# Preparing a selective state-space step: half-width products placed up to three steps ahead, the time-step bias inside a product, the skip term as a diagonal product

## The chip, the cores and the metric

One core of one Trainium2 chip runs the whole kernel. The metric is device time in microseconds. The kernel before took 3630.87 us in the median of three runs (3621.93, 3630.87 and 3643.5 us).

## What is computed

A one-layer tower over ids of shape 2 x 2048: embedding (256 wide) and 16-head attention, then `h = h + mamba(layernorm(h))`, then `h = h + ffn(layernorm(h))`. The change lies in the second part, the Mamba block, which runs once forward and once over the reversed sequence and adds the two:

```python
xh, z = jnp.split(x @ in_w.T, 2, axis=-1)                  # 512 channels each
xc = silu(conv_b + sum(xp[:, k:k + L, :] * conv_w[:, k] for k in range(4)))
dt, Bm, Cm = split(xc @ xproj_w.T)                         # 16, 16, 16
delta = softplus(dt @ dt_w.T + dt_b)
deltaA = exp(einsum('bld,dn->bldn', delta, -exp(A_log)))
deltaBu = einsum('bld,bln->bldn', delta * xc, Bm)
h = dA * h + dBu;  y = einsum('bdn,bn->bd', h, c)           # scan over the sequence, 16 states
y = (ys + xc * D_param) * silu(z);  return y @ out_w.T
```

All of it is float32.

## The kernel before

The program has four parts one after the other: embedding and projections, attention, `attention_out_and_mamba`, and `mamba_out_and_ffn`. Only the third is touched. Its second block is the state-space stage.

**Work units.** The stage has 16 *steps*: two directions, two batch rows, four chunks of 512 positions. A step has 64 *tiles* (slots), tile t = 4n + i for state n (16) and channel group i (4 groups of 128 channels). For each tile, ScalarE writes `da` = exp(delta * A) (line 1282) and a quarter of `bu` (line 1267: the transposed `delta*xc` scaled by B, one 128x512 block of positions; the fourth block of every second state is made by VectorE, line 1303). TensorE transposes `bu` back into PSUM (`inject`, line 1211, four 128-column transposes). VectorE runs the scan (line 1322). GpSimd multiplies the result by C (line 1187). TensorE adds this to `ps_y` by four accumulating transposes (`add`, line 1223), four tiles later (`LAG`).

**Preparation of later steps.** Between tiles, the same engines prepare the next steps in *fills* of a two-bank PSUM buffer `ps_a`: XH (input projection to xh, line 816, 4 fills of two 512-column products), CONV (taps as diagonal products, line 834, 4 fills of three), PROJ (line 838, four products), BT (transposes of B), DELTA (the 16-row time-step product, line 847, 4 fills), Z (line 821, 4 fills of two), DUT (transposes of delta*xc, line 853, 4 fills), YT (transposes of the gated output, line 826). Each fill takes the bank of the fill two places before it in `order`, and waits until that bank has been evacuated (`evacuated`, lines 763 to 771): by VectorE for CONV and DELTA, by ScalarE for the others. VectorE adds the last tap (`take_conv`, line 932); ScalarE takes SiLU of xc and of z (`silu_x`, `silu_z`, with a table load before and after) and the softplus: VectorE first writes min(x + bias, 20) (`cap`, line 941), ScalarE takes Exp and Ln (lines 906, 908), VectorE joins max(x + bias, that) (line 948). GpSimd makes delta*xc (`make_du`, line 801) and the skip term xc*D (line 1196), which TensorE adds by four transposes (line 1230).

**The order is written out by hand.** `PE_AT`, `ACT_AT`, `DVE_AT` and `DU_AT` (lines 714 to 728) say after which tile of the running step each piece for the next step is issued on each engine; a slot below 0 lies a step earlier (slot k - 64 u). All engines run in order. What keeps them together: `inject(t)` waits for scan t-2 (two PSUM banks, line 1209), `da` has 9 buffers, `bu` three states (line 1266), `hs` 8, `g` 5. So ScalarE may run several tiles ahead of the scan and TensorE at most two. Pieces with a slot before the first tile run in a prologue, before the first scan.

Of the kernel before, what the change touches and what calls it, by code (L numbers as in the profile page):

```python
# [36 lines left out]
XPW = X_DT2 + R  # L37
# [582 lines left out]
NDA, NHS, NG, NBU = 9, 8, 5, 3  # L620
HB = DC - 1
LAG = 4
CQ = 2
CAP = 20.0


def attention_out_and_mamba(nc, sem, o_scr, wo, bo, h_scr, dirs, win_t, xp_t, dtw_t, xn_scr, y_scr, c_scr):

    with ExitStack() as ctx, ExitStack() as ctx_out, ExitStack() as ctx_steps:
# [15 lines left out]
        def where(s):  # L645
# [9 lines left out]
        cols = sb("cols", [P, 2, 3, ND], FP32)  # L655
        a_cur = sb("a_cur", [P, 2, ND, DS], FP32)
        taps = sb("taps", [P, 2, ND, DC - 1, P], FP32)
        xn = sb("xn", [P, 2, KD, CH], FP32)
        xh = sb("xh", [P, ND, HB + CH + HB], FP32)
        skip = sb("skip", [P, CH], FP32)  # L660
# [35 lines left out]
        capped, e_ok, ln_ok, halo_ok = s_("capped"), s_("e_ok"), s_("ln_ok"), s_("halo_ok")  # L696
# [11 lines left out]
        skip_ok, skipped = s_("skip_ok"), s_("skipped")  # L708
# [95 lines left out]
        def fill(s, j, part):  # L804
# [5 lines left out]
            if f >= NA and first:  # L810
                evacuated(nc.tensor, f - NA)
            if j < CONV:
# [3 lines left out]
                last = nc.tensor.matmul(bank, win[:, part, j * P:(j + 1) * P], xn[:, q, part], start=first, stop=final)  # L816
            elif Z <= j < DUT:
# [3 lines left out]
                last = nc.tensor.matmul(bank, xn[:, q, part, tb * P:(tb + 1) * P], win[:, part, DI:2 * DI], start=first, stop=final)  # L821
# [5 lines left out]
            elif j < YT:  # L827
# [783 lines left out]
```

## Time and profile before

| | |
|---|---|
| median of three runs | 3630.87 us |
| the profiled execution: its span (the page gives no other time of it) | 3653.6 us |
| state-space stage, first to last scan | 1684.2 to 3354.5 us |
| busy share of the whole span, TensorE / VectorE / ScalarE / GpSimd | 91% / 79% / 76% / 43% |
| one full step (the sixth) | 104.0 us |

The page of the profile gives busy time and the costliest groups of instructions. A timeline row is a start, a length, engine, line, operation, output<-input and, in brackets, the idle time before it with what ended it. "x3" is the number of instructions merged into one row. Matmul lengths are modelled and overlap; the distance of two starts is the better measure.

### The profile page before, as it was taken

The numbers are of one execution on the slowest core, as the hardware profiler recorded it, in microseconds if no ns is written. First come the engines' busy times: TensorE is split into PE (matmuls) and PEld (weight loads), VectorE is DVE, ScalarE is ACT, GpSimd is POOL, SyncE is SP. The second block draws the span as 40 slices with busy tenths as digits, with TensorE's granted clock in tenths as the row PEclk, the third lists the DMA queues.
The fourth block names the chain that finished last, engine by engine and source line by source line (L and its number), as shares of the span: only waits on it lengthen the run. The fifth ranks groups of instructions, "written<-read, shape, count | busy, mean of one in ns | idle before, by whom it ended". The sixth has DMA issues, their size and how long they took to land. (4 is left out here: it accounts for less than half of the span.)

```text
span 3653.6 us, 69996 instructions
## 1 busy us (share of the span) xinstructions
PE 3330.3 (91%) x23969; PEld 1934.0 (53%) x23969; DVE 2898.1 (79%) x2810; ACT 2784.4 (76%) x4727; POOL 1569.7 (43%) x1443
## 2 busy tenths in 40 slices
PE   7699999999999999788999999999998999986798
PEld 4333333333333333355766667777676777765554
DVE  2689999799989999255888988898888888897121
ACT  2178888688888888617899989888998898896233
POOL 3100000000000000005898988988888889897000
PEclk9689999799999999889999999999999999999899
DMA  5420220202020200141111111111111111112322
GB/s 171 104 38 5 41 30 14 40 5 39 6 40 5 40 5 7 38 142 36 47 59 59 53 59 47 64 64 59 58 49 58 48 59 59 53 53 81 117 75 81
DMA packets 95178, 192.41 MB, mean 53 GB/s; under 512 B 17856, under 2 KB 32992, under 8 KB 93344
## 3 DMA queue, kind: packets, MB, share of 16 engines
q1 hardware_dynamic: 79440, 170.08, 16.9%
q10 hardware_dynamic: 13904, 14.03, 1.2%
q0 software_dynamic: 1536, 4.20, 0.5%
q8 instruction: 202, 3.31, 0.4%
q14 instruction: 96, 0.79, 0.1%
HBM read 136.63 MB, written 51.12 MB: 51 GB/s over the span
## 5 line engine op out<-in xcount | busy, mean ns | idle before, releaser
L1187 POOL TENSOR_TENSOR m_g<-m_hs,m_cb 128x512 f32<-128x512 f32 x1024 | 1302.1, 1292 | 191.2 <-DVE m_hs L1322 182.1
L575 DVE TENSOR_REDUCE a_mx<-a_ps_m 128x2 f32<-128x1024 f32 x1024 | 1242.0, 1224 | 91.3 <-PE a_ps_m L433 69.0
L551 ACT ACTIVATE a_probs<-a_ps_s 128x512 f32<-128x512 f32 x2048 | 1111.4, 596 | 204.4 <-PE a_ps_s L463 151.4
L1322 DVE TENSOR_TENSOR_SCAN m_hs<-m_da,m_carry,m_ps_x 128x512 f32<-128x512 f32 x768 | 952.9, 1268 | 128.2 <-PE m_ps_x L1211 89.9
L433 PE MATMUL a_ps_m<-a_k,a_q 48*128 48x512 f32 x2048 | 773.0, 470 | 34.5 <-DMA a_q<-q_scr 20.0
L463 PE MATMUL a_ps_s<-a_q,a_k 50*128 50x512 f32 x2048 | 775.7, 459 | 12.7 <-issue 5.6
L1211 PE MATMUL m_ps_x<-m_ident,m_bu 128*128 128x128 f32 x4096 | 640.7, 280 | 106.6 <-DVE m_hs L1322 96.3
L1211 PEld LDWEIGHTS m_ps_x<-m_ident,m_bu 128*128 128x128 f32 x4096 | 490.5, 143 | 442.6 <-issue 331.4
L1282 ACT ACTIVATE m_da<-m_delta,m_a_cur 128x512 f32<-128x512 f32 x1024 | 722.6, 711 | 0.5 <-DVE m_hs L1322 0.4
L1267 ACT ACTIVATE m_bu<-m_dut,m_bt 128x512 f32<-128x512 f32 x896 | 639.2, 714 | 109.9 <-PE m_ps_x L1211 106.8
L470 PE MATMUL a_ps_o<-a_probs,a_v 128*32 128x256 f32 x8192 | 667.7, 398 | 8.7 <-ACT a_o L538 8.2
L1223 PE MATMUL m_ps_y<-m_ident,m_g 128*128 128x128 f32 x4096 | 631.7, 278 | 8.4 <-POOL m_g L1187 6.2
L463 PEld LDWEIGHTS a_ps_s<-a_q,a_k 50*128 50x128 f32 x2048 | 316.7, 189 | 451.7 <-ACT a_probs L551 303.7
L407 POOL TENSOR_TENSOR a_neg_rows<-a_neg_col,a_neg_rows 16x128 fp32r<-16x128 f32 x32 | 14.4, 451 | 1247.1 <-ACT a_neg_rows L532 1247.1
L1223 PEld LDWEIGHTS m_ps_y<-m_ident,m_g 128*128 128x128 f32 x4096 | 489.8, 143 | 17.8 <-POOL m_g L1187 15.5
L470 PEld LDWEIGHTS a_ps_o<-a_probs,a_v 128*32 128x32 f32 x8192 | 163.6, 108 | 385.9 <-issue 217.1
L1322 DVE TENSOR_TENSOR_SCAN m_hs<-m_da,m_ps_x 128x512 f32<-128x512 f32 x256 | 304.0, 1210 | 71.4 <-PE m_ps_x L1211 57.1
L433 PEld LDWEIGHTS a_ps_m<-a_k,a_q 48*128 48x128 f32 x2048 | 311.2, 193 | 55.7 <-DVE a_mx L575 33.9
L834 PE MATMUL m_ps_a<-m_xh,m_taps 128*128 128x512 f32 x384 | 195.0, 594 | 1.6 <-ACT m_xh L874 1.6
L1420 PE MATMUL ffn_ps_h<-ffn_wo,ffn_y 128*128 128x256 f32 x512 | 116.4, 389 | 25.6 <-DMA ffn_h<-h_scr 25.6
L816 PE MATMUL m_ps_a<-m_xn,m_win 128*128 128x512 f32 x256 | 133.6, 612 | 6.4 <-PEq L982 5.1
L801 POOL TENSOR_TENSOR m_du<-m_delta,m_xc 128x512 f32<-128x512 f32 x64 | 82.6, 1312 | 131.8 <-DVE m_delta L948 131.8
(136 smaller groups left out, 2360.0 us busy)
## 6 DMA issues: line engine op xcount, KB each, us to landing
m_cb<-c_scr SPq DMA_DIRECT2D x128, 512.0 KB, 3.6
y_scr<-m_ysb SPq DMA_DIRECT2D x16, 1024.0 KB, 6.7
ffn_y<-y_scr SPq DMA_DIRECT2D x16, 1024.0 KB, 10.2
a_k<-k_scr SPq DMA_DIRECT2D x96, 128.0 KB, 6.7
a_q<-q_scr SPq DMA_DIRECT2D x96, 128.0 KB, 9.0
q_scr<-p_partsq SPq DMA_DIRECT2D x16, 512.0 KB, 3.3
k_scr<-p_partsk SPq DMA_DIRECT2D x16, 512.0 KB, 3.3
m_xn<-xn_scr SPq DMA_DIRECT2D x16, 512.0 KB, 5.0
```

Of the source, the lines that this page charges most:

```text
L433: nc.tensor.matmul(ps_m[:, i % MR], q_st[row:row + KQ, buf, c, pair, st * P:(st + 1) * P], k_st[row:row + KQ, buf, pair, tc * CH:(tc + 1) ...
L463: nc.tensor.matmul(turned(HG * t + HEADS.index(h)), k_st[row:row + KQM, buf, h // 2, t * P:(t + 1) * P], q_st[row:row + KQM, buf, c, h // ...
L470: last = nc.tensor.matmul(ps_o[h * VW:(h + 1) * VW, cols], v_st[:, buf, t, h], probs[:, t % PR, h, cols], start=t == 0 and half == 0, stop ...
L551: nc.scalar.activation(probs[:, t % PR, HEADS[j]], turned(i), ACT.Exp, scale=float(DK) ** -0.5).then_inc(exped, 1)
L575: nc.vector.reduce_max(mx[:, i:i + wide], ps_m[:, b:b + wide], AX.X).then_inc(m_maxed, 1)
L834: last = nc.tensor.matmul(bank, taps[:, z, dt, DC - 1 - back], xh[:, dt, start:start + CH], start=first, stop=final)
L1187: nc.gpsimd.tensor_tensor(g[:, t % NG], hs[:, t % NHS], cb[:, quarter % 2, n % CQ], ALU.mult).then_inc(g_ok, 1)
L1211: last = nc.tensor.transpose(ps_x[:, t % NX, tb * P:(tb + 1) * P], bu[:, (s * DS + n) % NBU, tb, i * P:(i + 1) * P], ident[:, :])
L1223: last = nc.tensor.matmul(ps_y[:, i, tb * P:(tb + 1) * P], g[:, t % NG, tb * P:(tb + 1) * P], ident[:, :], is_transpose=True, start=n == 0 ...
L1267: nc.scalar.activation(bu[:, m % NBU, tb], dut[:, s % 2, tb], ACT.Copy, scale=bt[:, s % 2, tb, n:n + 1]).then_inc(bt_ok, 1)
L1282: nc.scalar.activation(da[:, t % NDA], delta[:, q, i], ACT.Exp, scale=a_cur[:, z, i, n:n + 1]).then_inc(da_ok, 1)
L1322: nc.vector.tensor_tensor_scan(hs[:, t % NHS, rev], da[:, t % NDA, rev], ps_x[:, t % NX, rev], carry[:, n, i:i + 1] if p else 0.0, ALU.mul ...
```

## The change

- XH, CONV, PROJ and Z products of 512 columns become pairs of 256 columns, the first half of the bank and then the second, each part with its own slot. DELTA stays whole, and has 17 rows: a ones row in `proj` (made by the Identity evacuation with a bias column `ones`) meets `dt_b` as a row of `wdt`.
- XH is placed three steps ahead (slots 50 to 63 of step s-3), CONV two steps ahead (slots 33 to 49 of step s-2), SiLU of xc with it (slot 56 of step s-2, together with the SiLU of z of the running step), PROJ at slots 0 to 3, DELTA at 9 and 14, Z and DUT from 20 to 37.
- `cap` is gone: ScalarE takes Exp straight from the two PSUM banks; the join is max(min(softplus, 44), x).
- The skip term is no GpSimd work: TensorE multiplies xc by a diagonal matrix `skip_d` and accumulates into `ps_y`, at tiles 8, 10, 13 and 15 of the loop. VectorE builds `skip_d` twice in the whole stage.
- VectorE makes the fourth `bu` block of 12 of the 16 states instead of 8.
- The load of xn for step s+3 is issued behind the C loads of quarter 6; a load for step 2 leads SyncE's queue in the second block. Constants come in 18 transfers instead of 16.

```diff
-XPW = X_DT2 + R
+XPW = X_DT2 + R + 1
...
+HALF = CH // 2
+LIMIT = 44.0
...
-CAP = 20.0
...
-        cols = sb("cols", [P, 2, 3, ND], FP32)
+        cols = sb("cols", [P, 2, 2, ND], FP32)
         a_cur = sb("a_cur", [P, 2, ND, DS], FP32)
+        ones = sb("ones", [P, 1], FP32)
...
-        skip = sb("skip", [P, CH], FP32)
+        skip_d = sb("skip_d", [P, ND, P], FP32)
...
-        PE_AT = {XH: (-12, -11), XH + 1: (-6, -5), XH + 2: (-4, -3), XH + 3: (-2, -1),
-                 CONV: (2, 3, 4), YT: (5,), CONV + 1: (7, 8, 9), YT + 1: (10,), CONV + 2: (11, 12, 13), YT + 2: (14,),
-                 CONV + 3: (16, 17, 18), YT + 3: (19,), Z: (21, 22), PROJ: (25, 26, 27, 28),
-                 Z + 1: (29, 30), BT: (31,), Z + 2: (33, 34),
-                 DELTA: (37,), DELTA + 1: (37,), DELTA + 2: (44,), DELTA + 3: (44,),
-                 Z + 3: (50, 51), DUT: (54,), DUT + 1: (55,), DUT + 2: (56,), DUT + 3: (57,)}
-        SILU, SOFTPLUS = FILLS, FILLS + 2
-        ACT_AT = {XH: -6, XH + 1: 0, XH + 2: 2, XH + 3: 4, YT: 13, YT + 1: 18, YT + 2: 22, YT + 3: 25, SILU: 26,
-                  Z: 28, PROJ: 33, Z + 1: 35, BT: 36, Z + 2: 39, SOFTPLUS: 44, SOFTPLUS + 1: 50,
-                  Z + 3: 56, DUT: 59, DUT + 1: 60, DUT + 2: 61, DUT + 3: 62}
+        PE_AT = {XH: (-78, -77, -76, -76), XH + 1: (-75, -74, -73, -73), XH + 2: (-72, -71, -70, -69), XH + 3: (-68, -67, -66, -65),
+                 CONV: (-31, -30, -30, -29, -28, -28), CONV + 1: (-26, -26, -25, -24, -24, -23),
+                 CONV + 2: (-23, -22, -21, -21, -20, -19), CONV + 3: (-19, -18, -17, -17, -16, -15),
+                 PROJ: (0, 0, 1, 1, 2, 2, 3, 3), YT: (5,), YT + 1: (6,), BT: (7,),
+                 DELTA: (9,), DELTA + 1: (9,), DELTA + 2: (14,), DELTA + 3: (14,), YT + 2: (18,), YT + 3: (19,),
+                 Z: (20, 20, 21, 22), Z + 1: (22, 23, 24, 24), DUT: (25,), Z + 2: (26, 26, 27, 27), DUT + 1: (28,),
+                 Z + 3: (29, 30, 31, 31), DUT + 2: (32,), DUT + 3: (37,)}
+        SILU, SOFTPLUS = FILLS, FILLS + 1
+        ACT_AT = {XH: -70, XH + 1: -67, XH + 2: -63, XH + 3: -59, PROJ: 9, YT: 11, YT + 1: 12, BT: 13,
+                  SOFTPLUS: 15, SOFTPLUS + 1: 20, YT + 2: 24, YT + 3: 25, Z: 28, Z + 1: 30, DUT: 31, Z + 2: 34, DUT + 1: 35,
+                  Z + 3: 37, DUT + 2: 38, DUT + 3: 43, SILU: 56}
         JOIN = FILLS
-        DVE_AT = {CONV: 4, CONV + 1: 9, CONV + 2: 13, CONV + 3: 18,
-                  DELTA: 37, DELTA + 1: 38, JOIN: 42, JOIN + 1: 43,
-                  DELTA + 2: 44, DELTA + 3: 45, JOIN + 2: 48, JOIN + 3: 49}
-        DU_AT = {43: (0, 1), 49: (2, 3)}
+        DVE_AT = {CONV: -27, CONV + 1: -22, CONV + 2: -18, CONV + 3: -14,
+                  JOIN: 12, JOIN + 1: 12, JOIN + 2: 17, JOIN + 3: 17}
+        DU_AT = {14: (0, 1), 19: (2, 3)}
         GATE_AT = 2
-        SKIP_AT = (2, 5, 8, 13)
+        SKIP_AT = (1, 2, 1, 2)
...
-            found = [(u, j) for j, k in at.items() for u in range(STEPS + 2) if (u - 1) * TILES + k == slot]
+            found = [(u, j) for j, k in at.items() for u in range(-1, STEPS + 2) if (u - 1) * TILES + k == slot]
...
-            return m % 2 == 1
+            return m % 4 != 0
+
+        def scaled_by_dve(m):
+
+            return sum(by_dve(x) for x in range(m + 1))
 
         def scaled_by_act(m):
 
-            return (m + 1) * NTB - (m + 1) // 2
+            return (m + 1) * NTB - scaled_by_dve(m)
...
+            half, k = divmod(part, max(parts[j] // 2, 1))
+            begin, end = k == 0, k == parts[j] // 2 - 1
+            t0, t1 = half * HALF, (half + 1) * HALF
...
-                last = nc.tensor.matmul(bank, win[:, part, j * P:(j + 1) * P], xn[:, q, part], start=first, stop=final)
+                last = nc.tensor.matmul(bank[:, t0:t1], win[:, k, j * P:(j + 1) * P], xn[:, q, k, t0:t1], start=begin, stop=end)
-                last = nc.tensor.matmul(bank, xn[:, q, part, tb * P:(tb + 1) * P], win[:, part, DI:2 * DI], start=first, stop=final)
+                last = nc.tensor.matmul(bank[:, t0:t1], xn[:, q, k, tb * P:(tb + 1) * P], win[:, k, DI + t0:DI + t1], start=begin, stop=end)
-                last = nc.tensor.matmul(bank, taps[:, z, dt, DC - 1 - back], xh[:, dt, start:start + CH], start=first, stop=final)
+                last = nc.tensor.matmul(bank[:, t0:t1], taps[:, z, dt, DC - 1 - back], xh[:, dt, start + t0:start + t1], start=begin, stop=end)
-                last = nc.tensor.matmul(bank[0:XPW], wxp[:, z, part], xc[:, q, part], start=first, stop=final)
+                last = nc.tensor.matmul(bank[0:XPW, t0:t1], wxp[:, z, k], xc[:, q, k, t0:t1], start=begin, stop=end)
...
-                rows = slice(X_DT2, X_DT2 + R) if dt % 2 else slice(X_DT, X_DT + R)
+                rows = slice(X_DT2, X_DT2 + R + 1) if dt % 2 else slice(X_DT, X_DT + R + 1)
...
-                nc.scalar.activation(proj[:, q], bank[0:XPW], ACT.Copy).then_inc(taken, 1)
+                nc.scalar.activation(proj[:, q], bank[0:XPW], ACT.Identity, bias=ones[0:XPW]).then_inc(taken, 1)
...
-            nc.scalar.wait_ge(capped, s * ND + half * 2 + 2)
-            nc.scalar.activation(delta[:, s % 2, dts], delta[:, s % 2, dts], ACT.Exp).then_inc(e_ok, 1)
+            f = number[s, DELTA + half * 2]
+            assert f % NA == 0
+            nc.scalar.wait_ge(filled, f + 2)
+            if s >= 2 and half == 0:
+                nc.scalar.wait_ge(du_ok, (s - 1) * len(DU_AT))
+            nc.scalar.activation(delta[:, s % 2, dts], ps_a[:, :, :], ACT.Exp).then_inc(e_ok, 1)
             nc.scalar.wait_ge(e_ok, s * 2 + half + 1)
             nc.scalar.activation(delta[:, s % 2, dts], delta[:, s % 2, dts], ACT.Ln, bias=1.0).then_inc(ln_ok, 1)
 
         def act_stage(s, j):
 
             if j == SILU:
-                if s < STEPS:
-                    silu_x(s)
-                if s:
+                if s + 1 < STEPS:
+                    silu_x(s + 1)
+                if s >= 1:
                     silu_z(s - 1)
                 nc.scalar.preload_act_table_set("natural_log_exp_and_others")
             elif j >= SOFTPLUS:
-                if s < STEPS:
+                if 0 <= s < STEPS:
...
-                nc.vector.wait_ge(summed, (s - 1) * TILES)
+                nc.vector.wait_ge(skipped, (s - 1) * ND)
+                nc.vector.wait_ge(du_ok, (s - 1) * len(DU_AT))
...
-        def cap(s, dt):
-
-            q, f = s % 2, number[s, DELTA + dt]
-            if s >= 2 and dt == 0:
-                nc.vector.wait_ge(du_ok, (s - 1) * len(DU_AT))
-            nc.vector.wait_ge(filled, f + 1)
-            nc.vector.tensor_scalar(delta[:, q, dt], ps_a[:, f % NA], cols[:, where(s)[0], 1, dt:dt + 1], CAP, ALU.add, ALU.min
-                                    ).then_inc(capped, 1)
-
         def join(s, dt):
 
             q, f = s % 2, number[s, DELTA + dt]
             nc.vector.wait_ge(ln_ok, s * 2 + dt // 2 + 1)
-            nc.vector.scalar_tensor_tensor(out=delta[:, q, dt], in0=ps_a[:, f % NA], scalar=cols[:, where(s)[0], 1, dt:dt + 1],
-                                           in1=delta[:, q, dt], op0=ALU.add, op1=ALU.max).then_inc(delta_ok, 1)
+            nc.vector.scalar_tensor_tensor(out=delta[:, q, dt], in0=delta[:, q, dt], scalar=LIMIT, in1=ps_a[:, f % NA],
+                                           op0=ALU.min, op1=ALU.max).then_inc(delta_ok, 1)
 
         def dve_stage(s, j):
 
+            if not 0 <= s < STEPS:
+                return
             if j >= JOIN:
                 join(s, j - JOIN)
-            elif j >= DELTA:
-                cap(s, j - DELTA)
...
+                    nc.sync.dma_start(wdt[first + R:first + R + 1, z], w["dt_b"].rearrange("(o n) -> o n", o=1)).then_inc(w_in, 16)
...
+        def make_skip(z):
+
+            if z == 0:
+                nc.vector.tensor_tensor(ones[:, :], ident[:, X_DT + R:X_DT + R + 1], ident[:, X_DT2 + R:X_DT2 + R + 1], ALU.add).then_inc(ones_ok, 1)
+            for dt in range(ND):
+                last = nc.vector.tensor_scalar(skip_d[:, dt], ident[:, :], cols[:, z, 1, dt:dt + 1], None, ALU.mult)
+            last.then_inc(skip_made, 1)
...
+                load_xn(2)
                 store_c(0)
                 load_c(0, 0)
                 for s in range(STEPS):
                     load_c(s, 1)
-                    if s + 2 < STEPS:
-                        load_xn(s + 2)
-                    if s == STEPS // 2 - 2:
+                    if s == STEPS // 2 - 3:
                         load_win_x(1)
                     for h in range(2, DS // CQ):
                         load_c(s, h)
-                        if h == 6 and s + 1 < STEPS:
+                        if h == 3 and s + 1 < STEPS:
                             store_c(s + 1)
+                        if h == 6 and s + 3 < STEPS:
+                            load_xn(s + 3)
...
-                    if n == SKIP_AT[i]:
-                        if s or i:
-                            pool.wait_ge(skipped, s * ND + i)
-                        nc.gpsimd.tensor_scalar(skip[:, :], xc[:, s % 2, i], cols[:, where(s)[0], 2, i:i + 1], None, ALU.mult).then_inc(skip_ok, 1)
...
-                    if n == SKIP_AT[i] + 1:
-                        pe.wait_ge(skip_ok, s * ND + i + 1)
+                    if n == SKIP_AT[i]:
+                        pe.wait_ge(skip_made, where(s)[0] + 1)
                         for tb in range(NTB):
-                            last = nc.tensor.matmul(ps_y[:, i, tb * P:(tb + 1) * P], skip[:, tb * P:(tb + 1) * P], ident[:, :],
-                                                    is_transpose=True, start=False, stop=False)
+                            last = nc.tensor.matmul(ps_y[:, i, tb * P:(tb + 1) * P], xc[:, s % 2, i, tb * P:(tb + 1) * P],
+                                                    skip_d[:, i], start=False, stop=False)
...
-                        for part in range(DC):
+                        for part in range(2 * ND):
...
-                for slot in range(-2 * TILES, 0):
+                act.wait_ge(ones_ok, 1)
+                for slot in range(-3 * TILES, 0):
...
+                    if t == LAST // 2:
+                        dve.wait_ge(skipped, STEPS // 2 * ND)
+                        make_skip(1)
```

## Rows read from the trace of the kernel before

**Rows 1.** Page: the span, and busy time by engine.
```profile
span 3653.6 us, 69996 instructions
PE 3330.3 (91%) x23969; PEld 1934.0 (53%) x23969; DVE 2898.1 (79%) x2810; ACT 2784.4 (76%) x4727; POOL 1569.7 (43%) x1443
```

**Rows 2.** Line 1322 (the scan): durations, first and last start, what ended VectorE's idle time.
```profile
L1322 DVE TENSOR_TENSOR_SCAN m_hs<-m_da,m_carry,m_ps_x x768: 1244/1270/1283, 1788.5 to 3354.5; 128x512 f32<-128x512 f32 x192
L1322 DVE TENSOR_TENSOR_SCAN m_hs<-m_da,m_ps_x x256: 1185/1214/1222, 1684.2 to 3056.5; 128x512 f32<-128x512 f32 x128
...
  PE m_ps_x L1211: 147.0, 246
  ACT m_da L1282: 32.8, 33
```

**Rows 3.** Timeline of two slots with an XH product, TensorE and VectorE.
```profile
2203.75 0.60 PE L1211 MATMUL m_ps_x<-m_ident,m_bu 128*128 128x128 f32 x4
...
2204.48 1.22 DVE L1322 TENSOR_TENSOR_SCAN m_hs<-m_da,m_ps_x 128x512 f32<-128x512 f32 x1 [0.52 <-PE m_ps_x L1211]
...
2204.62 1.02 PE L816 MATMUL m_ps_a<-m_xn,m_win 128*128 128x512 f32 x2
...
2205.48 0.60 PE L1211 MATMUL m_ps_x<-m_ident,m_bu 128*128 128x128 f32 x4
```

**Rows 4.** Stretches (start:end, length, busy by engine, clock): the sixth step; its slots 24-31, 40-47.
```profile
2210.10:2314.10 104.00, 96.07 (x638) 72.46 (x637) 93.03 (x88) 94.59 (x152) 94.21 (x89) 1.00 0.17 57
2247.90:2262.40 14.50, 13.15 (x84) 9.59 (x84) 10.52 (x10) 14.47 (x22) 12.82 (x13) 1.00 0.12 37
2274.30:2287.70 13.40, 10.61 (x72) 7.90 (x72) 12.98 (x15) 11.80 (x18) 12.65 (x13) 1.00 0.12 43
```

**Rows 5.** The same view: slots 40-47 one step later, and the step before the last.
```profile
2378.30:2394.30 16.00, 13.46 (x72) 10.23 (x72) 14.25 (x14) 12.11 (x18) 13.11 (x13) 0.79 0.10 36
3164.10:3265.40 101.30, 92.22 (x622) 70.86 (x621) 92.30 (x88) 92.36 (x147) 91.75 (x87) 0.98 0.16 53
```

**Rows 6.** Timeline, slots 38 to 45 of the seventh step: VectorE, GpSimd, TensorE.
```profile
2376.45 0.72 DVE L941 TENSOR_SCALAR m_delta<-m_ps_a,m_cols 128x512 f32<-128x512 f32 x1
2377.09 3.61 DVE L1322 TENSOR_TENSOR_SCAN m_hs<-m_da,m_carry,m_ps_x 128x512 f32<-128x512 f32 x3
...
2379.96 2.52 POOL L1187 TENSOR_TENSOR m_g<-m_hs,m_cb 128x512 f32<-128x512 f32 x2
...
2380.62 2.14 DVE L1303 TENSOR_SCALAR m_bu<-m_dut,m_bt 128x512 f32<-128x512 f32 x1
...
2384.09 0.63 PE L1211 MATMUL m_ps_x<-m_ident,m_bu 128*128 128x128 f32 x4 [2.04 <-DVE m_hs L1322]
...
2388.47 1.11 PE L1211 MATMUL m_ps_x<-m_ident,m_bu 128*128 128x128 f32 x4
```

**Rows 7.** Timeline, the SiLU block on ScalarE and the scan after it.
```profile
2349.12 1.28 ACT L894 ACT_TABLE_LOAD   x1
...
2354.80 1.28 ACT L917 ACT_TABLE_LOAD   x1
2356.10 0.72 ACT L1282 ACTIVATE m_da<-m_delta,m_a_cur 128x512 f32<-128x512 f32 x1
...
2356.91 2.65 DVE L1322 TENSOR_TENSOR_SCAN m_hs<-m_da,m_carry,m_ps_x 128x512 f32<-128x512 f32 x2 [0.85 <-ACT m_da L1282]
...
2357.34 0.71 ACT L1282 ACTIVATE m_da<-m_delta,m_a_cur 128x512 f32<-128x512 f32 x1
```

**Rows 8.** TensorE timeline: the longest idle time of a full step, in the eleventh.
```profile
2824.45 1.09 PE L1211 MATMUL m_ps_x<-m_ident,m_bu 128*128 128x128 f32 x4 [3.77 <-DVE m_hs L1322]
```

**Rows 9.** Line 1303 (VectorE's copies into `bu`): shortest, median and longest, in ns.
```profile
L1303 DVE TENSOR_SCALAR m_bu<-m_dut,m_bt x128: 457/646/3946, 1686.5 to 3347.3; 128x512 f32<-128x512 f32 x128
```

**Rows 10.** Groups of 1700 to 3200 us: the skip term on GpSimd.
```profile
L1196 POOL TENSOR_SCALAR m_skip<-m_xc,m_cols 128x512 f32<-128x512 f32 x56 | 88.2, 1574 | 0.0
```

**Rows 11.** TensorE timeline of the prologue: the four CONV fills of step 0.
```profile
1634.05 10.54 PE L834 MATMUL m_ps_a<-m_xh,m_taps 128*128 128x512 f32 x24 [0.78 <-ACT m_xh L874]
```

More of the change, by code:

```diff
@@ L695, in attention_out_and_mamba @@
         z_ok, x_ok, delta_ok, du_ok = s_("z_ok"), s_("x_ok"), s_("delta_ok"), s_("du_ok")
-        capped, e_ok, ln_ok, halo_ok = s_("capped"), s_("e_ok"), s_("ln_ok"), s_("halo_ok")
+        halo_ok = s_("halo_ok")
         c_out, c_in = s_("c_out"), [s_("c_in0"), s_("c_in1")]
@@ L707, in attention_out_and_mamba @@
         h_stored, x_stored = [sem("o_hs0"), sem("o_hs1")], [sem("o_xs0"), sem("o_xs1")]
-        skip_ok, skipped = s_("skip_ok"), s_("skipped")
+        skip_made, skipped = s_("skip_made"), s_("skipped")
+        ln_ok, e_ok, ones_ok = s_("ln_ok"), s_("e_ok"), s_("ones_ok")
         bt_dve, zero_ok = s_("bt_dve"), s_("zero_ok")
@@ L831, in fill @@
                     nc.tensor.wait_ge(taken, takes[s, XH + ND - 1])
-                back = part + 1
+                back = k + 1
                 start = HB + back if z else HB - back
-                last = nc.tensor.matmul(bank, taps[:, z, dt, DC - 1 - back], xh[:, dt, start:start + CH], start=first, stop=final)
+                last = nc.tensor.matmul(bank[:, t0:t1], taps[:, z, dt, DC - 1 - back], xh[:, dt, start + t0:start + t1], start=begin, stop=end)
             elif j == PROJ:
@@ L965, in load_constants @@
                 nc.sync.dma_start(conv_w[:, z], w["conv_w"].rearrange("(k p) c -> p k c", p=P)).then_inc(w_in, 16)
-                for i, name in enumerate(("conv_b", "dt_b", "D")):
+                for i, name in enumerate(("conv_b", "D")):
                     nc.sync.dma_start(cols[:, z, i], w[name].rearrange("(k p) -> p k", p=P),
@@ L1081, in _ @@
                         root(n)
-                act.wait_ge(w_in, 16 * 16)
+                act.wait_ge(w_in, 16 * 18)
                 nc.scalar.activation(a_cur[:, :], a_cur[:, :], ACT.Exp).then_inc(a_exp, 1)
@@ L1124, in _ @@
                     if n == 2:
-                        dve.wait_ge(w_in, 16 * 16)
+                        dve.wait_ge(w_in, 16 * 18)
+                        make_skip(0)
                         make_taps()
@@ L1206, in inject @@
                     pe.wait_ge(bt_ok, scaled_by_act(s * DS + n))
-                    pe.wait_ge(bt_dve, (s * DS + n + 1) // 2)
+                    pe.wait_ge(bt_dve, scaled_by_dve(s * DS + n))
                     if t >= NX:
@@ L1304, in turn @@
                                             ).then_inc(bt_dve, 1)
-                for slot in range(-2 * TILES, 0):
+                for slot in range(-3 * TILES, 0):
                     for u, j in due(DVE_AT, slot):
@@ L1326, in _ @@
                     for u, j in due(DVE_AT, t):
-                        if u < STEPS:
-                            dve_stage(u, j)
+                        dve_stage(u, j)
                     if i == 1 and by_dve(s * DS + n + 1) and s * DS + n + 1 < STEPS * DS:
```

## The prediction, made before the change was run

> **What bounds the kernel now.** I read the page first: a span of 3653.6 us, TensorE busy 91% [rows 1]. The change touches the state-space stage alone, so the next view is the scan's own line. Its first start is at 1684.2 us and its last at 3354.5 us [rows 2]: 1670 us for 1024 tiles, 1.63 us per tile. Yet three scans in a row take 3.61 us [rows 6], 1.17 us from start to start. VectorE waits 147.0 us for `inject` and 32.8 us for `da` [rows 2]. Then the stretches: the sixth step lasts 104.0 us, with TensorE busy for 96, VectorE for 93, ScalarE for 95 and GpSimd for 94 us [rows 4]. Four engines are nearly full at once, so what counts is which of them is late in which slot.
>
> **A rule for one slot, and its check.** In a slot with an XH product TensorE goes from one inject to the next in 2205.48 - 2203.75 = 1.73 us [rows 3]. It does four equal pieces in it: inject, add, and two product instructions of 512 columns. One piece (512 columns, or four transposes) is 0.434 us. VectorE's slot is 1.18 us; an operation that reads PSUM adds 0.64 us (2376.45 to 2377.09) [rows 6], taken as 0.68 with its semaphore and 0.60 for a gate; a copy adds 0.46 [rows 9]. Inject starts when TensorE is through the slot before and scan t-2 has ended (0.2 us later, estimated from scan 42's end at 2383.87, a start of 2382.68 plus 1.19, to the inject at 2384.09 [rows 6]). A scan starts 0.73 us after its inject (2203.75 to 2204.48) [rows 3]. I walked both tables of slots through this rule. For the kernel before the walk gives 101.2 us a step, and 13.0 us for slots 24-31 and 12.6 us for slots 40-47. Measured are 104.0, 14.5 and 13.4 us [rows 4]. So 2.8 us of a good step are waits that the rule doesn't have; slots 40-47 take 16.0 us where a copy is held and the clock falls to 0.79 on average [rows 5]. From 1788.5 [rows 2] to 3164.1 us [rows 5] thirteen full steps take 105.8 us each.
>
> **The steady step, part by part.** *Half products and new slots.* A product of 256 columns is one piece in place of two; the number of pieces stays the same. TensorE's pieces per slot of the changed kernel are 4 4 4 4 2 3 3 2.6, then 4 6 4 2 2 4 6 4, 2 2 3 3 4 3 4 3, 4 3 4 4 3 3 3 4, 3 3 4 3 4 3 4 3, 4 4 3 4 3 4 3 4, 3 3 3 3 4 3 3 4 and eight times 3. *Skip.* Four GpSimd operations of 1.57 us [rows 10] go, 6.3 us a step. They lie beside the scan, and GpSimd's queue only becomes shorter: nothing on the path, but it was cover for nobody either. In their place the diagonal product isn't a transpose and costs two pieces and not one, four times: TensorE goes from 92.4 to 94.1 us of pieces. *Cap.* Four VectorE operations of 0.68 us go (2.7 us), with two waits of ScalarE; Exp then reads PSUM, for which I take the same time. *Copies.* Four more, 4 x 0.46 = 1.8 us on VectorE; ScalarE gets 4 x 0.61 = 2.5 us back. *Bias row and ones.* One row more in a product of 512 columns, Identity for Copy: nothing to pay, between a gain of 0 and 0.1 us a step. *Loads.* xn for step s+3 leaves SyncE behind quarter 6 (about slot 41) and is wanted at slot 50: 13 us of cover. Should that cover go, inject waits for the load. The sum by the walk: 98.2 us, 3.0 less than before. The larger of the two engines' sums over every eight slots gives 96.6, and slot by slot without any running ahead 105.2: those are the ends.
>
> **Waits that the change adds.** *SiLU.* The SiLU block holds ScalarE from 2349.12 to 2356.10, 7.0 us [rows 7], and the scan behind it waits for `da`. Before, it sits at slot 26, with 1.5 us of the excess. Now it sits at slot 56, amid the XH fills. XH+2 begins at slot 56 on TensorE and takes XH's bank, which ScalarE evacuates at slot 58, behind the block. ScalarE reaches slot 56 no earlier than inject 51 (its `bu` buffers), about 2.1 us after scan 49 ends; it adds 7.0 for the block, 2.4 for two slots of 1.22 us (two exponentials stand 1.24 us apart, 2356.10 and 2357.34 [rows 7]) and 0.7 for halo and evacuation, 12.2 us. TensorE comes to that fill 8.6 us after the same moment. It waits 3.6 us, and `inject(57)` and all adds are queued behind it; of these I count 3.4 on the scan. *Banks.* Z+3 at slot 29 takes Z+2's bank, evacuated at slot 34: 0.5 us. *Copies against GpSimd.* With GpSimd in its products back to back, a copy took 2.14 us and not 0.46 [rows 6]; the longest took 3.95 [rows 9]. The Trainium skill, page "SBUF — State Buffer", section "SBUF: two separate sides", has it that whoever starts first holds the shared port pair for one whole instruction; by that the term would be at most 1.3 us for each held copy, while this trace has copies held longer, and the measurement decides. GpSimd's backlog now follows `make_du` at tiles 14 and 19, with copies at 17 and 21: between 0 and 3.4 us a step, taken as 2.0. *Clock.* After 3.77 us without a product TensorE came back with an inject of 1.09 us in place of 0.60 [rows 8]: the half clock, 1.2 GHz. After 2.04 us the same came some microseconds on [rows 6]. So the 3.6 us at slot 56 is likely followed by such a time, on slots of three pieces with nothing to spare: 3.4 to 7 us at half rate lose 1.7 to 3.4, taken as 2.5, and 0.5 for drops at other places. The sum is 98.2 + 3.4 + 0.5 + 2.0 + 3.0 = 107.1 us a step against 105.8: +1.3 us.
>
> **Both ends of the stage.** The prologue now has CONV of step 1 and XH of step 2 before the first scan. Four CONV fills took 10.5 us [rows 11], four XH fills are 16 pieces, 6.9 us; two caps before two softplus runs save about 3 us, and a second SiLU block (2.6 us and two table loads of 1.28 us) is half hidden: +16 us, bounds +8 and +22. At the other end, the step before the last but one has no XH, the one before the last neither XH nor CONV. It takes 101.3 us before [rows 5]; without the stall at slot 56 I put both 5 us below: -10. Thirteen full steps, 13 x 1.3 = +17, +16, -10: **+23 us.** The constants and `skip_d` are under 1 us. The profiled execution becomes 3677; it stands 23 us above the median of 3630.87, so against the median the prediction is **3654 us**.
>
> **The rivals.** *Evened slots win* (faster): ScalarE comes to slot 58 in time, or VectorE is so late there that nothing waits; then the step is 98.2 + 0.4 (`da`) + 0.5 + 2.0 = 101.1, 4.7 us below before, 13 x -4.7 + 6 = -55: 3576 us. For it speaks that TensorE's waits are the largest item [rows 2]; against it the order of the queue, which is fixed. It holds from an evacuation that comes within 1 us of the fill. *Stall without the clock*: 107.1 - 3.0 = 104.1, 13 x -1.7 + 6 = -16: 3615 us. One drop in two steps gives no change. *GpSimd's backlog decides* (slower): every copy at 17, 21 and 25 is held by two products, 3 x 1.7 = 5.1 in place of 2.0, and drops follow there too: 111 us, +5 x 13 + 6 = +71, 3702 us. *It doesn't do what it says*: halves that cost more than one piece, for twice the weight loads. Transposes change weights every 128 columns at 0.109 us, so I give this 2 in 100, and it adds to the slower side.
>
> **Chances.** About 0.5% (18 us) can be told from no change. Forecast 0.42 (its own range 3635 to 3685), evened slots 0.20, stall without the clock 0.23, backlog 0.13, halves 0.02. Faster takes the evened slots and 0.10 of the third; same takes 0.13 of the third and 0.14 of the forecast, whose range crosses 3649; slower the rest: 0.30, 0.27, 0.43. The range 3572 to 3700 leaves out the far ends of evened slots and of the backlog.
>
> **What would show it.** Right: a TensorE idle time above 3 us before the XH+2 product, ended by ScalarE's `m_xh`, in each full step; slots 50-63 above 21 us where the walk has 18.7; the granted clock down just after; VectorE's waits for `m_ps_x` well below 147 us outside it; GpSimd near 86% of a step; copies at slots 17 and 21 above 1 us; the first scan 16 us later after the block's start. Wrong: steps under 103 us with no such wait, or a stall at the DELTA fills (slots 9 and 14, six pieces each), where I count none beyond the pieces.

## The result, and the profile after

The changed kernel takes 3684.4 us (median of four runs, 3678.5 to 3688.0) against 3637.2 us for the kernel before, measured beside it: a ratio of 1.013, 95% interval 1.010 to 1.016. It is slower by 47 us. Three later series with 20, 31 and 31 executions of the kernel before have medians of 3629.9 to 3633.3 us; against those it is slower by 51 to 55 us. The forecast was slower, at 3654 us, 23 us above the kernel before: the direction came, at twice the forecast size.

The profiled execution has a span of 3682.8 us, 29 us above the one of before [rows 1]. Executions of the kernel before lie up to 37 us apart within one series (3616.7 to 3653.8 us), and the span of the profiled one was 23 us above the median. Below, steps of the stage are therefore compared with steps, and not spans with spans.

Even the steps of that one execution are high. z3, the kernel before with its products cut in halves (see the experiments), takes the same time as the kernel before, and its scans are, in its own trace:

```profile
L1327 DVE TENSOR_TENSOR_SCAN m_hs<-m_da,m_carry,m_ps_x x768: 1245/1270/1282, 1779.1 to 3331.5; 128x512 f32<-128x512 f32 x192
L1327 DVE TENSOR_TENSOR_SCAN m_hs<-m_da,m_ps_x x256: 1185/1214/1223, 1673.3 to 3035.5; 128x512 f32<-128x512 f32 x128
```

That is 1658.2 us from first to last scan, and 104.9 us a step in steps 2 to 13, where the trace of before has 1670.3 and 105.9 us. With z3's trace as the base, the length of prologue and stage gives, for each of the twelve other kernels of this document, the distance of its median from that of before within 9 us (the changed one: +48 us, measured +47). With the trace of before as the base, every one of them, z3 too, comes out too fast, by 7 to 21 us. So "105.9 us a step before" is about 1 us too high wherever it stands below.

The page of the changed kernel:

```profile
span 3682.8 us, 72505 instructions
PE 3330.2 (90%) x25249; PEld 2147.2 (58%) x25249; DVE 2897.1 (79%) x2819; ACT 2750.2 (75%) x4665; POOL 1484.4 (40%) x1379
```

TensorE has 1280 more matmul instructions and the same busy time [rows 1]; GpSimd has 85 us less. The scan's own line, now 1336, and what ended VectorE's idle time before it:

```profile
L1336 DVE TENSOR_TENSOR_SCAN m_hs<-m_da,m_carry,m_ps_x x768: 1244/1274/1283, 1804.1 to 3386.2; 128x512 f32<-128x512 f32 x192
L1336 DVE TENSOR_TENSOR_SCAN m_hs<-m_da,m_ps_x x256: 1184/1220/1223, 1698.1 to 3098.3; 128x512 f32<-128x512 f32 x128
...
  PE m_ps_x L1224: 184.5, 237
  POOL m_g L1204: 11.2, 25
  ACT m_da L1296: 7.3, 8
```

The wait for TensorE's inject was to be cut and grew instead, from 147.0 to 184.5 us; the wait for the exponentials nearly went, 32.8 to 7.3 us [rows 2]. First to last scan takes 1688.1 us in place of 1670.3. Of these 17.8 us, steps 2 to 13 (s = 1 to 12) carry 12 x 2.1 = 25.4 us, the first step 1.7, and the last three give 9.3 us back. Such means over steps 2 to 13 (108.0 us here, 105.9 before) are what "a step" means below. Against z3's trace a step is 3.1 us longer. The first scan is also late: 78.1 us after the first XH product, where it was 60.1.

The stretches of the sixth step (the whole, slots 24 to 31, slots 56 to 63), then slots 56 to 63 two steps later, and the step before the last:

```profile
2234.10:2342.00 107.90, 98.88 (x718) 87.96 (x717) 94.03 (x89) 92.45 (x148) 88.90 (x85) 0.97 0.17 60
2274.60:2288.30 13.70, 12.82 (x96) 11.56 (x95) 10.77 (x10) 12.26 (x22) 12.90 (x13) 1.00 0.12 39
2324.90:2342.00 17.10, 13.32 (x81) 11.96 (x80) 10.56 (x11) 16.14 (x28) 10.61 (x11) 0.80 0.09 32
2542.00:2558.20 16.20, 12.32 (x82) 11.02 (x81) 10.62 (x11) 16.16 (x28) 10.38 (x9) 0.89 0.10 33
3202.60:3299.40 96.80, 83.79 (x638) 71.44 (x636) 91.27 (x85) 89.23 (x142) 88.99 (x85) 1.00 0.15 56
```

Slots 56 to 63 take 17.1 us where the slot rule has 10.4. The timeline there, TensorE first, then ScalarE, then VectorE:

```profile
2324.47 0.60 PE L1236 MATMUL m_ps_y<-m_ident,m_g 128*128 128x128 f32 x4
2328.85 1.22 PE L826 MATMUL m_ps_a<-m_xn,m_win 128*128 128x256 f32 x2 [3.78 <-ACT m_xh L884]
2329.87 1.06 PE L1224 MATMUL m_ps_x<-m_ident,m_bu 128*128 128x128 f32 x4
...
2322.30 1.90 ACT L910 ACTIVATE m_zs<-m_zs 128x2048 f32<-128x2048 f32 x1
2324.21 1.28 ACT L931 ACT_TABLE_LOAD   x1
...
2328.20 0.60 ACT L884 ACTIVATE m_xh<-m_ps_a 128x512 f32<-128x512 f32 x1
...
2331.06 1.28 DVE L1336 TENSOR_TENSOR_SCAN m_hs<-m_da,m_carry,m_ps_x 128x512 f32<-128x512 f32 x1 [4.95 <-PE m_ps_x L1224]
```

Read it from the middle. ScalarE is still in the SiLU block until 2325.5, makes two slots of `bu` and `da`, and evacuates XH at 2328.20. TensorE is through its last add at 2325.07 (2324.47 + 0.60) and stands until 2328.85 before the XH+2 product, for XH's bank. It comes back with an inject of 1.06 us, at the half clock of 1.2 GHz, and VectorE has idled 4.95 us. The same idle time on TensorE, 3.77 to 3.88 us, is there in all 13 steps that have an XH product (the first to the thirteenth); over the kernel the XH line shows

```profile
  ACT m_xh L884: 111.9, 30
```

us and waits, products and weight loads counted both.

### The profile page after: what moved, and what is told of

Read it like the earlier page. It is cut to its first block and busy times, and to the rows that moved or that the text cites. A ratio compares the mean times of both kernels' runs of the same rounds, so it can differ in the third digit from the quotient of the medians.

```text
span 3682.8 us, 72505 instructions
## 1 busy us (share of the span) xinstructions
PE 3330.2 (90%) x25249; PEld 2147.2 (58%) x25249; DVE 2897.1 (79%) x2819; ACT 2750.2 (75%) x4665; POOL 1484.4 (40%) x1379
## 5 line engine op out<-in xcount | busy, mean ns | idle before, releaser
L1281 ACT ACTIVATE m_bu<-m_dut,m_bt 128x512 f32<-128x512 f32 x832 | 593.0, 713 | 215.8 <-PE m_ps_x L1224 215.0
L1296 ACT ACTIVATE m_da<-m_delta,m_a_cur 128x512 f32<-128x512 f32 x1024 | 711.7, 710 | 0.0
L826 PE MATMUL m_ps_a<-m_xn,m_win 128*128 128x256 f32 x512 | 157.8, 415 | 59.1 <-ACT m_xh L884 54.0
L844 PE MATMUL m_ps_a<-m_xh,m_taps 128*128 128x256 f32 x768 | 205.2, 382 | 6.3 <-DVE m_xc L947 5.2
L831 PE MATMUL m_ps_a<-m_win,m_xn 128*128 128x256 f32 x512 | 140.8, 390 | 16.5 <-ACT m_zs L896 13.6
L1317 DVE TENSOR_SCALAR m_bu<-m_dut,m_bt 128x512 f32<-128x512 f32 x192 | 148.6, 774 | 0.0
```

The source lines that it names most:

```text
L844: last = nc.tensor.matmul(bank[:, t0:t1], taps[:, z, dt, DC - 1 - back], xh[:, dt, start + t0:start + t1], start=begin, stop=end)
L1281: nc.scalar.activation(bu[:, m % NBU, tb], dut[:, s % 2, tb], ACT.Copy, scale=bt[:, s % 2, tb, n:n + 1]).then_inc(bt_ok, 1)
L1296: nc.scalar.activation(da[:, t % NDA], delta[:, q, i], ACT.Exp, scale=a_cur[:, z, i, n:n + 1]).then_inc(da_ok, 1)
```

## The experiments

**x1: the evacuation ahead of the block.**

```diff
-        ACT_AT = {XH: -70, XH + 1: -67,
+        ACT_AT = {XH: -73, XH + 1: -67,
```

> The changed kernel with one number altered: ScalarE evacuates the first XH fill at slot 55, ahead of the SiLU block at slot 56, and not at slot 58 behind it. Theory (the XH+2 product waits for that bank, and the half clock follows the wait): the TensorE idle time of 3.8 us at slot 56 falls under 1 us, no clock drop follows it, slots 56 to 63 go from 17.1 to about 11 to 12 us, a full step from 108.2 to about 102.5 us, and the kernel is about 13 x 5.7 = 74 us faster than the changed one: about 3610 us, 0.7% faster than the kernel before. Rival (ScalarE's exponentials behind the SiLU block end last in any case): the wait only changes its name to da, slots 56 to 63 stay above 15 us, 3670 us or more.

Measured: 3662.7 us, ratio to the kernel before 1.010 (1.007 to 1.014); a step goes from 108.0 to 106.55 us. TensorE's idle time stays at 3.4 us, now before an inject, and VectorE's only changes its name. Slots 55 to 57 of the sixth step, VectorE and then ScalarE:

```profile
2333.90 2.42 DVE L1336 TENSOR_TENSOR_SCAN m_hs<-m_da,m_carry,m_ps_x 128x512 f32<-128x512 f32 x2
2340.30 1.28 DVE L1336 TENSOR_TENSOR_SCAN m_hs<-m_da,m_carry,m_ps_x 128x512 f32<-128x512 f32 x1 [3.98 <-ACT m_da L1296]
...
2337.58 1.28 ACT L931 ACT_TABLE_LOAD   x1
2338.88 0.72 ACT L1281 ACTIVATE m_bu<-m_dut,m_bt 128x512 f32<-128x512 f32 x1
2339.50 0.71 ACT L1296 ACTIVATE m_da<-m_delta,m_a_cur 128x512 f32<-128x512 f32 x1
```

The expectation fell and its rival held. ScalarE works in order: evacuating at slot 55, it idles 2.48 us before the halo (which needs CONV's last evacuation, slot 50) and 1.24 us for the XH product, uses up its lead there, and begins the block while scan 53 runs, not scan 51. The block then starves the exponentials. So the bank was the wait that ended last, and right behind it stood the block's own length.

**y1: the block later, behind two evacuations.**

```diff
-        ACT_AT = {XH: -70, XH + 1: -67, XH + 2: -63, XH + 3: -59,
+        ACT_AT = {XH: -70, XH + 1: -68, XH + 2: -67, XH + 3: -59,
-                  ... SILU: 56}
+                  ... SILU: 60}
```

> The changed kernel with ScalarE's SiLU block at slot 60 and not 56, behind the evacuations of XH (58) and XH+1 (60); XH+2 is evacuated at slot 61 in place of 65. Theory (x1 showed that the block itself, 7.0 us, outlasts ScalarE's lead of five or six slots of 1.2 to 1.3 us, and that in-order evacuations before it only move the wait; what counts is the length of the scans that run beside the block and whether a bank hangs on it): the scans beside it are now those of slots 54 to 60, three pieces each, no XH bank waits behind the block, so the idle time falls from 3.8 to 1 to 2 us, the clock drop goes in most steps, a step is 103 to 104.5 us against 108.0, and the kernel takes 3625 to 3645 us. Rival (any place among slots of 1.3 us starves the scan alike): the wait moves to slot 60 or 61 with 3 us or more, a step stays above 106 us, 3660 us or more.

Measured: 3637.8 us, ratio 1.0005 (0.998 to 1.003), 103.6 us a step. As expected. One whole step, and its slots 56 to 63:

```profile
2230.30:2333.90 103.60, 96.23 (x717) 85.20 (x716) 94.05 (x88) 91.66 (x147) 88.82 (x84) 1.00 0.18 62
2321.30:2333.90 12.60, 11.23 (x83) 9.60 (x82) 10.48 (x10) 12.56 (x17) 10.58 (x11) 1.00 0.11 44
```

The clock stays at 1.00; 4.5 of the 17.1 us are gone, and no wait for `m_xh` is left on TensorE. What is left at the block is 1.64 to 2.03 us of VectorE's idle time at slot 61, for the exponentials. Three numbers in a table take back 4.3 us a step, more than the whole steady loss: this is the shown cause. Without it the change is neutral. How much of it is the block's place and how much the two evacuations ahead of it, no run separates; x1 shows only that one evacuation ahead of a block at slot 56 isn't enough.

**x3, x4, y2: the copies.** x3 is the changed kernel, y2 is y1, each with `return m % 2 == 1` in place of `m % 4 != 0`; x4 is the kernel before with the 12 copies and nothing else.

> The changed kernel with VectorE making 8 of the 16 copies a step, as before, and ScalarE the other 4. Theory (each of the four added copies costs VectorE its 0.46 us and a wait for GpSimd's port, 0.31 us on average, above all the 1.2 us at slot 5 and 1.1 us at slot 37, while ScalarE has room): a step is 1.0 to 2.5 us shorter, 16 to 40 us in all, 3645 to 3670 us. Rival (ScalarE is short of time, and the copies free it before the SiLU block): the stall at slot 56 grows and the kernel is the same as the changed one or up to 20 us slower.

> The kernel before with VectorE making 12 copies of 16, nothing else. Theory: four more copies cost VectorE 1.8 us a step and their waits about 1.2 us, of which half lies in slots that TensorE bounds: +1 to +2 us a step, 16 to 32 us slower than before. Rival (ScalarE's relief is worth more, since scans wait for its exponentials behind the SiLU block at slot 26): 0 to 20 us faster.

> y1 with 8 copies on VectorE in place of 12. Theory (x3 gave 2.7 us a step for the four copies, mostly at slots 5, 37 and 53): the two gains add, so 2 to 3 us a step below y1, 30 to 40 us in all, 3590 to 3610 us, faster than the kernel before by 0.6% to 1.1%. Rival (with more work ScalarE comes later to the block): less than 1 us a step below y1.

Measured: x3 3649.4 us, ratio 1.005 (1.003 to 1.008), 105.2 us a step, 2.7 less than the changed kernel: the theory held, a little above its 1.0 to 2.5. x4 3653.3 us, 1.007 (1.005 to 1.009), 23 us slower, as expected; its 106.6 us a step are 0.8 above the trace of before and 1.8 above that of z3, and only the second fits 23 us. y2 3653.9 us, 1.006 (1.004 to 1.008), 105.5 us a step, 1.8 *more* than y1: the expectation fell. The reason shows in slots 0 to 7: 12.9 us in x3, 15.5 us in y2 with the clock at 0.90.

```profile
2232.90:2245.80 12.90, 12.44 (x96) 10.94 (x95) 12.37 (x14) 11.57 (x20) 10.25 (x10) 1.00 0.25 82
```

(x3), and in y2

```profile
2331.20:2346.70 15.50, 12.76 (x90) 11.18 (x89) 12.65 (x14) 15.50 (x27) 12.09 (x13) 0.90 0.10 34
```

In y2 ScalarE is busy for all 15.5 us: it comes out of the block at slot 60 with no lead, and is late at its evacuation of PROJ, slot 9, whose bank TensorE wants for YT+1 at slot 6. In y2 TensorE waits for it (the line of the YT transposes, matmuls and weight loads counted both)

```profile
  ACT m_proj L892: 60.8, 28
```

or 2.1 to 2.3 us a step in all but one of the full steps, against 1.5 us in y1 and next to none in x3. The half clock follows in nine of the twelve steps 2 to 13. The three without it take 104.2 us, 0.5 us more than y1; the nine with it take 105.9 us. So most of what y2 loses is the clock. In x3 the stall at slot 56 stops everybody else and, as I read it, hands ScalarE its lead back. The same four copies on VectorE cost 2.7 us a step with the stall there and gain 1.8 us without it.

x3 also prices the clock. Two of its steps have the stall and no clock drop; slots 56 to 63 of one:

```profile
2533.30:2547.90 14.60, 10.73 (x82) 9.69 (x81) 10.32 (x9) 14.56 (x25) 9.88 (x8) 1.00 0.11 36
```

14.6 us at full clock, 16.0 to 16.3 where the clock was low for 3.4 us, and 17.1 us in the changed kernel where it was low for 6.8 us. So a drop costs 1.5 to 2.5 us there, and the stall alone about 4 (14.6 less the rule's 10.4).

**x2: halves in pairs.** x1 with both halves of a product in one slot, for example

```diff
-        PE_AT = {XH: (-78, -77, -76, -76), XH + 1: (-75, -74, -73, -73),
+        PE_AT = {XH: (-78, -78, -76, -76), XH + 1: (-75, -75, -73, -73),
```

and likewise for the other XH, CONV and Z products that were spread.

> The kernel of x1 with both halves of each XH, CONV and Z product put into one slot, as a whole product would lie (the pieces and their number are the same). Theory from the slot rule (98.9 against 98.2 us a step): the halves' own places are worth 0.7 us a step, 10 us in all, so 3620 us. Rival (the half products are what carries the change): slots of four pieces in runs cost 0.56 us each again, 3 us a step or more, 3655 us or above.

Measured: 3689.1 us, 26 us above x1, 108.1 against 106.55 us a step. That is 1.5 us a step, between the 0.7 of the theory and the 3 of the rival (both their times had counted on an x1 of 3610 us). Slots 16 to 55 take 0.8 us more together, which is the rule's 0.7. Another 0.6 us comes from clock drops at slot 7, in five of the twelve steps where x1 has none, and 0.4 us from slots 56 to 63. This prices the fine placement at 0.7 to 1.5 us a step, and doesn't settle more.

**z3: halves alone.** The kernel before with each product as two halves in the same slots.

> The kernel before with each XH, CONV, Z and PROJ product as two halves of 256 columns in the same slots, so that only the number of instructions changes. Theory (a half is half the time: the halves of the changed kernel stand 0.217 us apart): no change, within 0.3% of the kernel before. Rival (twice the weight loads cost time): 44 more loads of 0.05 us or more a step, 2 us a step or more, 35 us slower.

Measured: 3626.5 us, ratio 0.998 (0.996 to 1.000). No change: a half is half the time. The trace has 1024 more instructions than before, 64 a step and not the 44 expected, and no cost for their weight loads that can be told.

**z1 and z2: skip and cap alone, on the kernel before.** z1 has `skip_d` and its products at the old slots. z2 has the ones row, Exp from PSUM and the join with 44, at the old slots:

```diff
-            nc.scalar.wait_ge(capped, s * ND + half * 2 + 2)
-            nc.scalar.activation(delta[:, s % 2, dts], delta[:, s % 2, dts], ACT.Exp).then_inc(e_ok, 1)
+            nc.scalar.wait_ge(filled, f + 2)
+            banks = ps_a[:, ::-1, :] if f % NA else ps_a[:, :, :]
+            nc.scalar.activation(delta[:, s % 2, dts], banks, ACT.Exp).then_inc(e_ok, 1)
```

> The kernel before with the skip term as a diagonal product at the same slots, nothing else: 4 x 1.57 us of GpSimd a step go, TensorE has four pieces (1.7 us) more. Slot rule: 102.5 against 101.2, +1.3 us a step. GpSimd's shorter queue gives back up to 1 us at the held copies of slots 9 and 41. Theory: 0 to +1.3 us a step, the same as before to 20 us slower. Rival (GpSimd's backlog holds the copies and was the cause of the 2 us stalls at slot 41): 1 us a step or more faster, 15 us or more.

> The kernel before with the cap gone: the bias as a seventeenth row of the time-step product against a ones row, Exp straight from the two PSUM banks, the join as max(min(softplus, 44), x), at the old slots. Slot rule: 99.1 against 101.2, -2.0 us a step; and ScalarE no longer waits for VectorE at slot 44 (3.8 us of its idle time in one step). Theory: 2 to 4 us a step faster, 30 to 60 us in all, 3570 to 3600 us. Rival (those VectorE operations lie in slots that TensorE or ScalarE bounds): under 1 us a step, no change that can be told.

Measured: z1 3628.7 us, 0.999 (0.997 to 1.001), 105.0 us a step; z2 3632.4 us, 1.001 (0.998 to 1.004), 105.6 us a step. z1 is no change that can be told, as its theory allowed; its step is that of z3. In z2 the 30 to 60 us didn't come. A good part of it went into the copies, here line 1300; VectorE and GpSimd in one of four such steps:

```profile
L1300 DVE TENSOR_SCALAR m_bu<-m_dut,m_bt x128: 458/646/5819, 1662.9 to 3317.1; 128x512 f32<-128x512 f32 x128
```

```profile
2681.79 5.40 DVE L1300 TENSOR_SCALAR m_bu<-m_dut,m_bt 128x512 f32<-128x512 f32 x1
...
2681.97 2.49 POOL L1183 TENSOR_TENSOR m_g<-m_hs,m_cb 128x512 f32<-128x512 f32 x2
2684.42 2.48 POOL L802 TENSOR_TENSOR m_du<-m_delta,m_xc 128x512 f32<-128x512 f32 x2
```

A copy of 0.46 us stood through four GpSimd instructions in a row and ended when GpSimd was idle. Such a step has its slots 48 to 55 at 17.8 to 19.4 us and not 13; there are four of them and two in the trace of before, 1.0 us a step more, and 1.4 us more than in z3. That is half or more of the 2.0 us that the rule gives for the cap. The rest I can't place: slots 32 to 39 gained 0.8 us, slots 40 to 47 vary from 11.4 to 16.1 us with the clock drops in them, and no run separates these.

**v1, v2, v3: towards a better version.** v1 is y1 with `XH + 3: -62`; v2 is v1 with `Z + 2: 32` in place of 34; v3 is v2 with 8 copies.

> y1 with XH+3 evacuated at ScalarE's slot 2 and not 5. In y1 TensorE still waits 1.5 us before the transposes of YT at slot 5, whose bank is XH+3's. Theory: that wait goes, a step is 1.0 to 1.5 us below y1's 103.6 us, 102.1 to 102.6 us, 15 to 20 us in all: 3615 to 3625 us, 0.3% to 0.5% faster than the kernel before. Rival (the evacuation only displaces exponentials that slots 2 to 5 need): no change from y1.

> v1 with Z+2 evacuated at slot 32 and not 34, for the wait of 1.1 us at slot 29 (2.45 us where the slot rule has 1.30). Theory: slots 24 to 31 go from 13.6 to 12.3 to 12.6 us, a step is about 101.2 us, the kernel 3600 to 3610 us. Rival (ScalarE then waits for the Z+2 product and comes late elsewhere): under 0.5 us a step.

> v2 with 8 copies on VectorE in place of 12. In y2 the four copies' return to ScalarE cost 1.8 us a step, because ScalarE reached XH+3's evacuation at slot 5 late and TensorE's clock fell; here that evacuation is three slots earlier. Theory: slots 0 to 7 and 32 to 39 now show x3's gain, 1 to 2.5 us a step below v2, 3570 to 3590 us. Rival (ScalarE needs the relief wherever it catches up behind the block): equal to v2 or slower.

Measured: v1 3634.4 us, ratio 1.001 (0.998 to 1.003), 103.6 us a step; v2 3614.5 us, 0.994 (0.992 to 0.997), 102.5 us a step; v3 3643.4 us, 1.002 (1.000 to 1.005), 104.9 us a step. v1 changed nothing and its expectation fell: I had read the 1.5 us at slot 5 off the neighbour. TensorE waits there before YT+1, whose bank is PROJ's, as the line of the YT transposes in v2 says:

```profile
  ACT m_proj L892: 42.6, 28
  DVE m_delta L954: 19.7, 28
```

In v2 the part that was its own came: slots 24 to 31 went from 13.6 to 12.5 us, and a step is 1.1 us shorter. The 101.2 us a step and 3600 to 3610 us had counted on v1's gain too, and didn't come. Slots 24 to 31 of the sixth step:

```profile
2251.10:2263.60 12.50, 12.50 (x95) 11.48 (x94) 10.71 (x9) 12.28 (x21) 12.50 (x13) 1.00 0.14 43
```

v2 is faster than both kernels, by 0.6% than the one before. v3's expectation (3570 to 3590 us) fell as y2's did: it is 29 us slower than v2, TensorE again waits 2.1 to 2.2 us for PROJ's bank, and the half clock follows in nine of the twelve steps, which take 105.6 us where the other three take 102.9. PROJ's evacuation at slot 9 and the prologue, 84 to 85 us in y1 to v3, weren't tried.

## Why the prediction was right, and where its terms were off

The direction, the place of the stall, its releaser and its length were right for the reason given. The size wasn't: +47 us against +23, and 3684.4 us lies at the very end of the forecast's own range (3635 to 3685). Of the missing 24 us about 10 are steps that came out 0.9 us longer than forecast, 2 the prologue, and about 11 a base that was high: a step of 105.8 us taken from one execution, where z3's trace has 104.9.

- **The slot rule.** It gave 98.2 us for the changed table without waits (walked again, I get 98.0). In y1, which has no long stall, slots 8 to 15 and 32 to 55 are within 0.7 us of it for every eight. Slots 0 to 7 and 16 to 23 stay 0.8 and 0.9 us above it, slots 24 to 31 1.4 us (1.1 of it the bank of Z+2), and slots 56 to 63 2.3 us, behind the block. The pieces were right, also the two for each diagonal product (z1 has 16 instructions more a step), and halves cost nothing (z3).
- **The stall at slot 56.** Forecast: 3.6 us of idle time, named by place, bank and releaser; measured: 3.78 us, at that product, for `m_xh`. Its two legs hold as well: from the end of scan 49 (2315.95) to the end of XH's evacuation (2328.80) 12.9 us where 12.2 were forecast, and to TensorE's arrival (2325.07) 9.1 where 8.6 were. On the scan the stall is about 4.0 us and not 3.4. The prediction missed that the block was itself next in line (x1), and so its rival of evened slots was priced with 0.4 us for `da` where x1 waits 3.98 us and y1, the nearest to that rival, still 1.64 to 2.03. Its 101.1 us a step are 103.6 in y1.
- **The clock.** Taken as 2.5 us at slot 56, measured 1.5 to 2.5, in 13 of 13 steps with the stall. The 0.5 us for other places: drops at slot 7 in four of the twelve steps, 1.6 us each.
- **Bank of Z+2.** Mis-sized: 0.5 us forecast, 1.1 measured (v2).
- **Copies.** Taken as 2.0 us of waits a step. The longest copy is 1.6 us, but those at slots 5, 17 and 37 wait in every step (1.2, 1.4 and 1.1 us in the mean, where an unhindered one takes 0.46):

```profile
L1317 DVE TENSOR_SCALAR m_bu<-m_dut,m_bt x192: 456/650/1579, 1702.5 to 3379.6; 128x512 f32<-128x512 f32 x192
```

  I had looked behind `make_du` only. Twelve a step at 774 ns in the mean make 9.3 us, against 8 x 842 ns = 6.7 us before. How much of their 3.8 us of waiting lies where VectorE is what bounds the slot, no run tells. The Trainium skill, page "SBUF — State Buffer", section "SBUF: two separate sides", says that whoever starts first has the shared port pair for the whole instruction while the other blocks. Read as a wait of one instruction, about 1.3 us, that bounds all copies of this kernel, and falls short in z2, where one was held through four.
- **The sum.** 107.1 us forecast, 108.0 measured: the 13 full steps lose 27 us in all in place of 17, and 37 against z3's trace.
- **The ends.** Prologue +16 forecast, 18.0 measured. The last steps: -10 forecast, -9.3 measured, partly by luck, for the two steps named gave 2.4 and 4.5 us and not 5 each, and the very last one, not counted, gave 2.4. So the stage and its prologue account for +36 us by the trace of before, where +23 was forecast, and for +48 us by that of z3. The medians differ by 47, so the other 11 us lie most likely in the stage of the one execution of before that was profiled; one trace of it can't show that.
- **The signs that were named.** Idle time above 3 us at XH+2, ended by `m_xh`: yes. The clock down just after: yes. Slots 50 to 63 above 21 us: 24.4 to 25.8 us. VectorE's waits for `m_ps_x` below 147 us outside it: yes, the stall is 4.93 to 5.17 us in each of 13 steps, 66 us in all, which leaves 119. GpSimd at 86% of a step: 88.9 of 107.9 us, 82%. Copies at slots 17 and 21 above 1 us: at 17, and then at 5 and 37; at 21 in some steps only. The first scan 16 us later: 18. And the one sign against it, a stall at the DELTA fills: none.
- **Skip and cap.** "Nothing on the path" for the skip held (z1). Taking the cap off was entered at its full rule gain; alone it gives no change (z2).

## What to carry to other kernels

When pieces are spread evenly over short slots, the engine that runs ahead loses the cover for its longest uninterruptible block: let no buffer that another engine wants soon be released behind it (y1). A place where the slots beside it are long should cover it too, as at slot 26 of the kernel before, where the scan waited 0.85 us [rows 7]; no run here moved the block there in the changed kernel. Before moving work off an engine, ask what that engine's slack is with the present stalls gone, since a stall elsewhere may be what gives it its lead. After naming the wait that ends last, look up what would have ended next, or the fix only renames it. And a step measured in one execution is one sample: check it against a second trace before a forecast of 1 us a step is set on it.

## What was not expected of the hardware

A VectorE copy between SBUF tensors was held by GpSimd not for one instruction but for as long as GpSimd's instructions followed each other without a gap: 2.14 us over two [rows 6], 5.40 us over four (z2). And a time at half clock cost less where TensorE had slack: slots 40 to 47 of the kernel before took 12.8 to 13.4 us without a drop [rows 4] and 14.5 to 14.9 us with one of 6.8 us and no held copy, 1.1 to 2.1 us more, while the same drop over slots of three pieces with the stall cost 2.5 us.
